# Where one queue of a two-layer attention kernel sends its inputs: image and feature transfers spread over the slots, and the strip above tile 0 one slot earlier

## What is computed

```python
def _contextual(b, mask):
    raw_w, Hr, Wr = _extract_patches(b, 4, 2)          # 4x4 patches of the image, step 2
    f = b[:, :, ::2, ::2]
    w, Hs, Ws = _extract_patches(f, 3, 1)              # 3x3 patches at half resolution
    norm = jnp.sqrt(jnp.sum(w * w, axis=(2, 3, 4), keepdims=True))
    wn = (w / jnp.maximum(norm, 1e-4)).reshape(B, L, C * 9)
    yi = jnp.einsum('bpd,bld->blp', w.reshape(B, L, C * 9), wn) * mm
    yi = jax.nn.softmax(yi * 10.0, axis=1) * mm
    patches = jnp.einsum('blp,bld->bpd', yi, raw_w.reshape(B, L, C * 16))
    ...  # the patches are added into the output where they overlap, cropped, divided by 4

x = _contextual(x, mask0)
x = _contextual(x, mask1)
```

## Time and profile before

| | us |
|---|---|
| median of 3 runs (1452.59 to 1453.62) | 1453.11 |
| the profiled execution | 1459.86 |
| span of its instructions | 1457.9 |
| TensorE busy (84%) | 1228.7 |
| VectorE busy (82%) | 1192.9 |
| ScalarE busy (66%) | 955.6 |
| GpSimd busy (40%) | 587.7 |
| mean granted TensorE clock | 0.943 |

### The profile page before, as it was taken

One profiled execution on the slowest core, in us unless ns is written; L12 is line 12 of the kernel. 1 busy time (PEld: TensorE's weight loads), 2 busy tenths in 40 slices (PEclk: granted clock), 3 DMA queues, 4 the chain that ended last, 5 costly groups with the idle time before them and its releaser, 6 DMA issues.

```text
span 1457.9 us, 20011 instructions
## 1 busy us (share of the span) xinstructions
PE 1228.7 (84%) x4910; PEld 761.7 (52%) x4910; DVE 1192.9 (82%) x2539; ACT 955.6 (66%) x2657; POOL 587.7 (40%) x510
## 2 busy tenths in 40 slices
PE   5766898988898888888888888898888889788796
PEld 4545554655456654465445654455554565356444
DVE  4677989799898988878898888978979899898662
ACT  3768756776577765787566875767657866478431
POOL 1003543255332544236342454325533263434772
PEclk9987999999999999999999999999999999999898
DMA  4401473135722455225641257313472235322442
GB/s 76 73 1 57 120 149 88 43 99 118 151 78 64 106 116 132 65 77 129 122 113 37 81 128 149 88 42 98 117 147 81 63 108 108 94 68 81 132 139 57
DMA packets 179174, 138.35 MB, mean 95 GB/s; under 512 B 119602, under 2 KB 177010, under 8 KB 179058
## 3 DMA queue, kind: packets, MB, share of 16 engines
q1 hardware_dynamic: 178898, 136.57, 39.6%
q10 hardware_dynamic: 160, 0.50, 0.2%
HBM read 19.76 MB, written 13.11 MB: 23 GB/s over the span
## 4 chain that ended last, share of the span: by engine, by line
DVE 30%; PE 21%; issue 14%; ACT 13%; SPq 12%; DMA 8%; POOL 2%; DVEq 0%; ACTq 0%; POOLq 0%
PE psO L586 12%; DVE S L1028 8%; PE psG L534 6%; SPq L389 6%; ACT S L800 5%; DMA SH<-G 5%; DVE Z L1124 5%; DVE G L1100 5%; DVE G L988 4%; SPq L333 3%; SPq L377 3%; ACT G L811 2%; DVE G L983 2%; DMA SHJ<-G 2%; POOL G L1241 2%
## 5 line engine op out<-in xcount | busy, mean ns | idle before, releaser
L1241 POOL TENSOR_TENSOR G<-G,SH 123x492 f32<-123x492 f32 (+1 forms) x448 | 549.1, 1235 | 854.6 <-DMA SH<-G 853.3
L586 PE MATMUL psO<-Z,B 123*128 123x492 f32 (+2 forms) x1792 | 741.5, 545 | 63.4 <-DVE Z L1124 37.1
L586 PEld LDWEIGHTS psO<-Z,B 123*128 123x128 f32 x1792 | 345.6, 200 | 289.8 <-issue 159.1
L800 ACT ACTIVATE S<-S,nm 123x480 f32<-123x480 f32 (+3 forms) x560 | 308.9, 556 | 238.4 <-DVE nm L1034 238.2
L1028 DVE CUSTOM_DVE_ANT_0 S<-G,RB 123x492 f32<-123x492 f32 (+1 forms) x448 | 350.1, 786 | 29.6 <-ACT G L727 28.2
L534 PE MATMUL psG<-LH,HL 128*123 128x492 f16 (+2 forms) x1104 | 282.6, 366 | 87.8 <-DVE G L983 68.3
L811 ACT ACTIVATE G<-G,nb 123x492 f32<-123x492 f32 (+1 forms) x448 | 268.6, 644 | 94.2 <-DVE G L1100 92.6
L1124 DVE TENSOR_TENSOR Z<-G 123x984 f32<-123x984 f32 (+2 forms) x192 | 217.2, 1131 | 68.7 <-POOL G L1241 56.0
L1100 DVE SCALAR_TENSOR_TENSOR G<-G,RA,psB 123x492 f32<-123x492 f32 (+1 forms) x448 | 269.8, 644 | 0.3 <-issue 0.3
L534 PEld LDWEIGHTS psG<-LH,HL 128*123 128x123 f16 x1104 | 145.5, 140 | 215.6 <-DVE G L983 83.2
L549 PE MATMUL psG<-idn,G 123*123 123x123 f32 x672 | 110.4, 293 | 37.8 <-DVE G L1004 31.0
(11 more groups left out here) (85 smaller groups left out, 740.9 us busy)
## 6 DMA issues: line engine op xcount, KB each, us to landing
SH<-G SPq DMA_DIRECT2D x336, 214.8 KB
SH<-G SPq DMA_DIRECT2D x112, 89.2 KB
SH<-G SPq DMA_DIRECT2D x336, 19.2 KB
XP<-x SPq DMA_DIRECT2D x20, 280.0 KB, 6.1
XP<-mid SPq DMA_DIRECT2D x20, 280.0 KB, 5.9
HL<-LH SPq DMA_DIRECT2D x16, 246.5 KB, 4.1
mid<-OSB SPq DMA_DIRECT2D x48, 80.0 KB, 2.3
out<-OSB SPq DMA_DIRECT2D x48, 80.0 KB, 2.3
```

Source lines behind the costliest of these rows:

```text
L586: last = pe.matmul(psO[:, b, 0:n], B[:, o:o + 128], Z[:, 2 * (s % 2) + j, 0:n], start=t == 0, stop=t == TILES - 1)
L800: last = act.activation(y, y, ACT.Exp, bias=nm[:, k * TILES + t:k * TILES + t + 1], accum_out=sg[:, c:c + 1])
L1241: pool.tensor_tensor(g, g, SH[:, o % SFREE, 0:n], ALU.add).then_inc(y1_made, 1)
```

## The change

Three things change, all in SP's queue.

- The three feature loads are no longer issued together ahead of slot 3's shifts. One stands in each of slots 2, 3 and 4, behind that slot's shifts and strip. The wait for `b_made` stays ahead of the first.
- The six image loads are no longer issued together ahead of slot 9's shifts. One stands in each of slots 13 to 18, behind that slot's shifts and strip. The waits of `xp_read` stay ahead of the first. The feature layout of slots 10 and 11 now stands ahead of the image loads.
- `shift_strip` for the first pair of a chunk is called a slot further ahead: in slots 4, 11, 18 and 25 instead of 5, 12, 19 and 26. It stands behind that slot's shifts, and what it waits for is the same.

```diff
-            def load_features(u, w, src):
-                if u is not None:
+            def load_features(u, w, src, j):
+                if u is not None and j == 0:
                     sp.wait_ge(b_made, (u + 1) * PAIRS)
                     sp.sem_inc(sp_gate, 1)
-                load_rows(src, 1, feat_in)
+                load_rows(src, 1, feat_in, (j,))
...
-            def load_image(u, w, src):
-                if w is not None:
+            def load_image(u, w, src, a, j):
+                if w is not None and (a, j) == (0, 0):
                     xp_read(w)
-                else:
+                elif (a, j) == (0, 0):
                     sp.wait_ge(b_made, (u + 1) * PAIRS)
                     sp.sem_inc(sp_gate, 1)
-                for a in range(2):
-                    load_rows(src, a, image_in)
+                load_rows(src, a, image_in, (j,))
...
             def body(u, v, w, feat_src, image_src, dst):
                 for s in BODY:
-                    if s == 3 and w is not None:
-                        load_features(u, w, feat_src)
-                    if s == 9 and v is not None:
-                        load_image(u, w, image_src)
                     at = place(u, v, s + LEAD)
                     if at:
                         shift_pair(at)
-                    at = place(u, v, s + 2)
+                    at = place(u, v, s + 3)
                     if at and at[2] == 0:
                         shift_strip(at)
+
+                    if s in (2, 3, 4) and w is not None:
+                        load_features(u, w, feat_src, s - 2)
+                    if 13 <= s < 13 + 2 * STRIPS and v is not None:
+                        load_image(u, w, image_src, (s - 13) // STRIPS, (s - 13) % STRIPS)
```

More of the change, by code:

```diff
@@ L326, in _, with load_rows @@
         def _(sp):
-            def load_rows(src, a, done):
+            def load_rows(src, a, done, strips=range(STRIPS)):
                 rows = src.rearrange("c (h two) w -> two c h w", two=2)[1 - a]
                 v = XP[64 * a:64 * a + 64, :, :].rearrange("p (t j) w -> p j t w", j=STRIPS)
-                for j in range(STRIPS):
+                for j in strips:
                     lo, hi = max(TILES * j, 1 - a), min(TILES * (j + 1), HALF + 1 - a)
```

## The result

| | before | with the change | ratio, 95% interval |
|---|---|---|---|
| median, us | 1453.36 (4 runs) | 1414.93 (4 runs) | 0.9724 (0.9693 to 0.9755) |
| again, beside the last experiments | 1455.03 (9 runs) | 1418.15 (5 runs) | 0.9747 (0.9723 to 0.9771) |
| profiled execution | 1459.86 | 1412.9 | |

The change makes the kernel 38 us faster, 2.8%. The forecast was 1383 us, 70 us less than before, and the range 1360 to 1418. So the sign and the range held, and the size came out at just over half. TensorE's mean granted clock went from 0.943 to 0.953.

The account below looks back on a forecast made before the run. Neither TensorE (84% busy) nor DVE (82%) is full; time is lost where both stand, chiefly behind image loads, pair 13's shifts and POOL. Terms 52 + 11 + 7 = 70 us, from 1453.1 to 1383 us; range 1360 to 1418.

Parts of the forecast that it names:

- Image loads: Units 0 to 6, pair 13: DVE's wait for POOL goes, 41.7 us, plus 10.5 us of stretched work; 52 us in all.
- The blocking: DVE's sums beside POOL's bunched additions: 3.0 us a unit above normal, half taken back, 1.5 us x 7 = 10.5.
- its rival: The blocking moves with POOL's additions, so the stretched DVE work returns nothing: 60 us gained, 1394; chance 0.20.
- Feature loads and the strip of pair 7: Third load behind the strip adds 2.2 us of ACT wait; 1.4 of 2.73 us of DVE's strip wait come back.
- I take 45% of 25.2, 11 us: Strips a slot earlier, units 0 to 6: 11 of DVE's 25.2 us of strip waits come back; bounds -18 and 25.
- the strip's wait holds the next shifts: Rival at pair 16: shifts start 2.1 us later, covered by 7.8 us of slack, otherwise 1 to 3 us a unit; no chance given.
- The last unit: No scores or loads there; TensorE waits for the strip ahead of pairs 7, 14 and 21; 7 us gained, between 0 and 14.
- TensorE takes over (1415): Rival: DVE arrives early and finds TensorE behind; only 38.6 us return, strips and last unit give nothing; chance 0.17.

Follow-up runs that it names:

- feat3_early: Against the changed kernel, the third feature load stands right behind the second in slot 3, ahead of slot 4's shifts and the strip; 1403.75 us, ratio 0.9669.

## Why the prediction was right in its sign and half right in its size

**Image loads: predicted 52 us, measured 48.** Twice, with ratios 0.9669 and 0.9667. The path was as told: loads, shifts of pair 13, POOL, DVE. The step from pair 11 to 13 fell by 7.4 us a unit, and some 1 us came back at pairs 13 to 14.

**The blocking: between the forecast and its rival.** I had taken 1.5 of 3 us a unit as returned for good, 10.5 us in all; the rival had none of it returned. DVE's busy time for the same instructions was 1192.9 us before and, with the image loads alone, 1190.8 and 1181.9 in two executions. So 2 to 11 us of work went, beside 47 and 43 us of idling. The step from pair 12 to 13 fell, but its neighbours were stretched: from pair 11 to 14 DVE is busy 20.4 us a unit before and 20.3 and 19.4 with the image loads alone. The Trainium skill ("SBUF — State Buffer", Who interferes with whom) states that a DVE instruction with two SBUF inputs contends with a GpSimd instruction that reads SBUF; the count of long sums above agrees. Most of the 3 us moved to other instructions, and the scatter of 9 us between two executions leaves open whether the forecast or its rival was nearer.

**Feature loads and the strip of pair 7: the working held.** I had 2.2 us of wait for ACT; it was 1.3 to 2.3. I had 1.4 us come back at pair 7 in all; the two steps from pair 6 to 8 fell by 1.2 us (17.40 to 16.21), and by 0.8 in the second execution. What I did not ask is what they would have given apart: with the features spread and the strip left behind them the two steps fall by 1.9 to 2.6 us, and the wait that the strip puts on ACT costs 8 to 11 us of the total.

**The failed step is "I take 45% of 25.2, 11 us"**, the carrying over of pair 7 to all strips, together with the slack that was to cover the shifts behind them. Measured, the strips lose: alone 5 us, beside the two others 23 us. The strip waits of the earlier trace rows went entirely, but DVE's work became longer. Its busy time in us, for the same 2539 instructions, two numbers where there are two executions:

| | strips in the old slots | strips a slot earlier |
|---|---|---|
| loads as before | 1192.9 | 1212.6 |
| image loads spread | 1190.8, 1181.9 | 1217.3 |
| image and feature loads spread | 1173.3 | 1194.9, 1202.4 |

That is 20 to 35 us more work in each row, where two executions of one kernel differ by 8 to 9. With the strips alone DVE's idling fell from 265.0 to 239.0 us and its work rose by 19.7 (the two do not add up to the 5 us of the medians, as the profiled executions lie on opposite sides of theirs). The 1194.9 against 1192.9 of the result hide both effects: some 20 us of work were saved by spreading the loads and lost again by the strips.

Where it was lost differs. Behind pair 7 with the strips alone it is longer work; in the changed kernel it is the wait for ACT, 3.0 us of DVE's idling in that step. Behind pair 21, strips alone, DVE idles 0.6 us more and works 0.4 us longer. In the changed kernel the steps from pair 0 to 1 and from 15 to 16 are longer by 0.8 and 1.9 us. The load behind the strip accounts for 8 to 11 of the 23 us; the kernel without that wait (`feat3_early`) is 12 us behind the fastest one by the ratios, and 1.7 us a unit of that, 12 in seven, lie between pairs 13 and 16. The rival "the strip's wait holds the next shifts" had the place right, pair 16, and was covered by 7.8 us of slack. The slack held, no wait appeared, and the price came all the same, as longer work of DVE beside POOL's bunched additions. The same rival did not mention the load behind the strip.

**The last unit: predicted 7 us, between 0 and 14.** It is 3 us shorter in the trace (117.0 to 114.0). That is within the scatter named above, but over all traces its mean is 116.0 us in the five with the old place of the strip and 114.2 in the nine with the earlier one, so some 2 us seem real. Its strip waits fell from 15.6 to 4.0 us, and its waits for POOL (L1124) rose from 12.9 to 22.5: one wait took much of the other's place.

**TensorE takes over (1415)** gave the measured number for the wrong reason. DVE's waits for `psO` before the last unit rose from 1.4 to 9.3 us, so TensorE took at most about 8 us. The image loads alone, which feed TensorE just as early at that place, are 10 us faster than the changed kernel, and the version with features 23, so TensorE was not the bound.

The sum with the measured terms: 48 for the images, 13 for the features beside them, less 23 for the strips (the last unit's gain is in it), is 38 us. That the total stayed inside the range owes something to luck: the strips came out beyond the lower end of their own term, -18, and the features, which had no term of their own, gave 13.

## What to carry to other kernels

A transfer that is moved a slot ahead takes its waits along, and what is queued behind it may pay: ask of each instruction behind it who is waiting for it, here a load three calls further on and an engine that had no slack. A wait that stands ahead of an engine which is anyhow held by another is not worth its length; look at what that engine waits for in the next two instructions before counting it. Fewer waits with the same instructions need not mean a gain: compare the busy times too. When a change has several parts, time each alone and each left out: here one of three parts was worth more than all of them.

## What the runs showed of the hardware

- The same DVE sum takes 1.17 us or 2.04 to 2.11, by what POOL does beside it, and a step of 6.3 us grows to 8.3, with no wait of DVE in the trace. Which of DVE's instructions an addition meets seems to matter as much as how many additions there are; I have only the places where they met, and no run that varies this alone.
- A load of 240 KB alone in the queue landed 3.8 us after its issue began, and the six image loads of a unit sent one by one took 3.8 to 4.5 (unit 2); the last ones of six together took up to 8.0.
- Executions of one and the same program differ by some 10 us (1399.75 to 1411.29 for the image loads alone), so differences of 5 us between kernels needed both on one chip and five rounds, and some stay open.
